# Keys' pieces on VectorE in one run, and the last batch's first maxima turned one event later

## The reference

```python
latent = x @ Wc_down
q = (latent @ Wq_up).reshape(Bsz, Tlen, N_HEAD, HEAD_DIM)
kv = latent @ Wkv_up
k, v = (kv[..., :HEAD_DIM], kv[..., HEAD_DIM:])
att = jnp.einsum('bthd,bsd->bhts', q, k) * scale
att = jnp.where(causal[None, None], att, -jnp.inf)
att = jax.nn.softmax(att, axis=-1)
y = jnp.einsum('bhts,bsd->bthd', att, v).reshape(Bsz, Tlen, C)
```

## Time and profile before

| | us |
|---|---|
| median of 3 runs | 868.62 |
| lowest, highest | 868.59, 870.29 |
| profiled execution | 868.64 |
| its span | 866.9 |

### The profile page before, as it was taken

The page is one execution under the profiler, slowest core; times in us unless marked ns, Lnnn a source line. Parts: engine busy times, 40 slices in busy tenths (PEclk is TensorE's granted clock), DMA queues, the critical chain, the costliest instruction groups (busy, mean ns, idle before and its releaser), DMA issues. The chain is left out here.

```text
span 866.9 us, 20372 instructions
## 1 busy us (share of the span) xinstructions
PE 812.4 (94%) x5472; PEld 487.5 (56%) x5473; DVE 641.0 (74%) x2159; ACT 548.7 (63%) x1236; POOL 294.8 (34%) x547
## 2 busy tenths in 40 slices
PE   7989999999999999999999999379999999999993
PEld 3433333333333333333333348279999999999993
DVE  7899888988898989898988628745555555555552
ACT  4636667867677777677776766146666666666661
POOL 5412333244233432441233322033444444444211
PEclk9989999999999999999999999579999999999997
DMA  6204222321211111111153118930000100110000
GB/s 209 71 11 112 77 81 97 100 86 64 97 55 57 48 36 58 62 42 43 64 172 113 52 57 268 330 96 31 30 31 31 36 30 27 36 32 19 19 19 2
DMA packets 55764, 62.92 MB, mean 73 GB/s; under 512 B 13166, under 2 KB 47366, under 8 KB 55568
## 3 DMA queue, kind: packets, MB, share of 16 engines
q1 hardware_dynamic: 51952, 53.71, 19.2%
q0 software_dynamic: 3744, 8.40, 3.1%
HBM read 36.12 MB, written 9.57 MB: 53 GB/s over the span
## 5 line engine op out<-in xcount | busy, mean ns | idle before, releaser
L1192 ACT ACTIVATE W2s<-bank 128x512 f32<-128x512 f32 (+1 forms) x512 | 257.1, 572 | 117.2 <-PE bank L1084 115.0
L1252 DVE CUSTOM_DVE_ANT_0 room_kv<-bank,causal 128x384 bf16<-128x384 f32 (+3 forms) x512 | 220.7, 486 | 31.9 <-PE bank L1053 30.5
L1084 PE MATMUL bank<-W2s,room_kv 99*128 99x512 bf16 (+3 forms) x768 | 224.2, 330 | 4.5 <-ACT W1s L1192 3.0
L1053 PE MATMUL bank<-room_kv,W2s 96*128 96x512 bf16 (+3 forms) x768 | 218.5, 330 | 4.3 <-DVE R L1223 2.7
L1255 DVE TENSOR_REDUCE MP<-bank 128x1 f32<-128x512 f32 x256 | 162.8, 681 | 12.5 <-PE bank L1053 12.4
L1400 POOL TENSOR_SCALAR_AFFINE_SELECT W2s<-W2s 128x512 f32<-128x512 f32 x96 | 60.9, 635 | 286.5 <-ACT W2s L1192 284.3
L1084 PEld LDWEIGHTS bank<-W2s,room_kv 99*128 99x128 bf16 x768 | 67.9, 97 | 146.0 <-ACT W2s L1192 62.3
L1667 PEld LDWEIGHTS hp<-XNT,LT 128*128 128x128 f32 x1248 | 147.3, 194 | 3.3 <-DVE XNT L1744 1.4
L1667 PE MATMUL hp<-XNT,LT 128*128 128x128 f32 x1248 | 147.8, 277 | 1.0 <-DVE XNT L1744 1.0
L1675 PE MATMUL yp<-W2s,LT 128*128 x624 | 141.2, 379 | 0.6 <-DVE z L1755 0.6
L1101 PE MATMUL bank<-W2s,room_kv 128*32 128x512 f32 (+2 forms) x1152 | 129.4, 534 | 0.1
(11 more groups left out here) (189 smaller groups left out, 760.2 us busy)
## 6 DMA issues: line engine op xcount, KB each, us to landing
W2s<-W2s SPq DMA_DIRECT2D x160, 64.0 KB, 2.6
W1s<-in_L_ffn_W_dram SPq DMA_DIRECT2D x8, 1024.0 KB, 5.5
W2s<-in_L_ffn_W_dram SPq DMA_DIRECT2D x8, 1024.0 KB, 7.3
Y<-in_L_attn_x_dram SPq DMA_DIRECT2D x8, 512.0 KB, 7.7
Y<-W1s SPq DMA_DIRECT2D x32, 128.0 KB
W1s<-den_rows SPq DMA_DIRECT2D x16, 256.0 KB
LT<-in_L_attn_x_dram SPq DMA_DIRECT2D x8, 512.0 KB, 7.7
x_rows<-LT SPq DMA_DIRECT2D x8, 512.0 KB, 5.2
```

What stands on the lines that cost most here:

```text
L1053: last = pe.matmul(bank[:, at:at + w], Q[0:NR, g, i // BW, h, i % BW * P:(i % BW + 1) * P], K[b % 2][0:NR, k * NQ:k * NQ + w], start=True, ...
L1084: last = pe.matmul(dst[:, i, :], K[b % 2][0:KR, j * P:(j + 1) * P], Q[0:KR, g, c, h, off:NQ], start=True, stop=True)
L1192: act.activation(PR[t % RB][:, heads[0]:heads[-1] + 1, off:NQ], unit_of(ST[(NU * n + u) % STB], s), ACT.Exp, scale=SCALE).then_inc(exp_don ...
L1252: op = dve.tensor_tensor_reduce(junk[:, done % 2, at:at + w], src, causal[:, NQ - w:NQ], 1.0, LOWEST, ALU.add, ALU.max, dst)
```

## The change

Two things are changed. For a keys' piece, VectorE does the residual at the piece's own event, straight behind the cast, instead of after the maximum that follows; the wait for its own cast moves behind the copy of the values. `DONE` counts the releases accordingly. And for the last batch (blocks 13, 14 and 15 as seen by the maxima, which run during blocks 12, 13 and 14), the first half's "m" is placed one event later in the table.

```diff
-            marks.append((NM * r + SET_LAST[c] + (MLAT if r else FIRST_MLAT[c]) + 0.5, ("m", r, c)))
+            marks.append((NM * r + SET_LAST[c] + (MLAT + (r > NG * (B - 1) and not c) if r else FIRST_MLAT[c]) + 0.5, ("m", r, c)))
...
-    if EVENTS[event][0] != "piece":
+    if EVENTS[event][0] != "piece" or EVENTS[event][2] == "k":
         DONE.append(event)
-    if event and EVENTS[event - 1][0] == "piece":
+    if event and EVENTS[event - 1][0] == "piece" and EVENTS[event - 1][2] != "k":
         DONE.append(event - 1)
...
             def residual(k):
                 _, b, name = EVENTS[k]
-                dve.wait_ge(part1, piece_no(b, name) + 1)
+                rows = rows_of(name)
                 dve.wait_ge(part3, piece_no(b, name))
-                rows = rows_of(name)
                 if name == "k":
                     dve.tensor_copy(R1[KEPT:KEPT + rows, :], ring[k % RING][0:rows, :]).then_inc(v_copied, 1)
+                dve.wait_ge(part1, piece_no(b, name) + 1)
                 dve.tensor_tensor(R1[0:rows, :], ring[k % RING][0:rows, :], parts(name)[0], ALU.subtract)\
                    .then_inc(ring_done, 1)
...
-                    if k and EVENTS[k - 1][0] == "piece":
+                    if (kind, b) == ("piece", "k"):
+                        residual(k)
+                    if k and EVENTS[k - 1][0] == "piece" and EVENTS[k - 1][2] != "k":
                         residual(k - 1)
```

## The result

| | kernel before | changed kernel |
|---|---|---|
| median, us | 868.59 | 863.80 |
| lowest, highest (5 runs each) | 868.11, 870.29 | 863.27, 865.36 |
| profiled execution, its span | 868.64, 866.9 | 863.80, 862.0 |

Over all sets of runs in this study the changed kernel's median is 864.5 (21 runs) and that of the kernel before 868.5 (72 runs), 4.0 us apart; why one set of five shows 4.8 and another 3.2 is most of what the experiments are about.

What follows compares the result with a forecast made beforehand. TensorE was taken to set the attention's pace. Keys' pieces 2.25 us plus last batch 1.30 us make 3.55, so 868.64 - 3.55 = 865.1 us; range 864.0 to 867.0 us.

Steps and rivals of the forecast that it cites:

- TensorE sets the pace of the attention, and what it gains is passed on: Attention part: TensorE idles less than any other engine, and everything behind the attention moves up as a whole.
- Keys' pieces, 2.25 us: Keys' piece in three batches: earlier subtraction frees the bank, transpose 0.95 us earlier, of which TensorE gains 0.75 each.
- the ends: Bounds of the gain per keys' piece: upper the full 0.95 us (2.85 together), lower 0.35 (1.05 together).
- VectorE's 0.35: Keys' piece: VectorE gains 0.35 us, all that counts if VectorE rather than TensorE sets the pace behind it.
- Last batch, 1.30 us: Last batch's three later transposes: work moved ahead fills 0.44, 0.42 and 0.44 us of TensorE's wait for GpSimd.
- The lower end of the range, 864.0: Whole kernel: time no lower than 864.0 us, the figure with both parts at their upper ends.
- rival 1: VectorE sets the pace behind the keys' piece: 1.05 + 1.30 = 2.35 us gained, 866.3 us; chance 0.11.
- rival 2: Last batch: the later transpose fills nothing, a matmul ahead of it waits instead; 2.25 us gained, 866.4 us; chance 0.06.
- rival 3: Keys' piece gains nothing lasting, through the displaced maximum's bank or a later wait; 1.30 us gained, 867.3 us; chance 0.11.
- Rival 4: Keys' pieces and last batch both reach their upper ends: 2.85 + 1.78 = 4.63 us gained, 864.0 us; chance 0.03.
- rival 5: Slower: new spacing brings a granted-clock fall of 1.72 us at each of three keys' pieces, 870.3 us; chance 0.05.

## Why the prediction was right in kind and too small

- **TensorE sets the pace of the attention, and what it gains is passed on.** Right. What the six places gained was still there at the last copy, and the experts' work moved up with it.
- **Keys' pieces, 2.25 us.** Right: 2.27. The order of starts came as worked out (copy 0.71 behind the cast, transpose 0.97 earlier against the cast, second matmul behind it late by 0.2), and so did the choice between the ends: TensorE leads, VectorE's 0.35 isn't what counts.
- **Last batch, 1.30 us.** The mis-sized term of the sum: 1.50. It priced the two matmuls that move ahead at 0.22 each, as the gap in front of a matmul of their own kind, and it put the transpose, had it not waited, 0.22 behind the maximum's matmul. But what moves up is the product with the values, and it stands 0.31 behind a maximum's matmul (417.25 to 417.56 in the kernel before) and only 0.15 behind a transpose (413.57 to 413.72). So 0.53 us are filled at the first and third place, measured 0.54 and 0.54. At the second, the transpose that no longer waits stands 0.31 behind the maximum's matmul, not 0.22, so its stall was 0.33 and not 0.42. From the maximum's matmul that was the last ahead of the transpose to the product it took 1.32 us (443.48 to 444.80) and now takes 0.91 (439.64 to 440.55): measured 0.40. That is near the 0.42 of the sum only because two errors nearly cancel: the stall was 0.09 us less, and the new order by itself saves 0.08.
- **The lower end of the range, 864.0: the step that failed.** The term of 0.20 alone would not have done it: with the measured 3.74 us the sum gives 864.9, inside the range. What failed is that the range put the clock at nothing on the way down. It took the profiled execution of 868.64 as its start and moved the terms of the edits alone in rivals 1 to 4; the clock entered only as rival 5, a fall that the change would bring. But the execution from which the sum starts itself held a fall, shown in the earlier trace rows, that some executions don't have and others have as a longer first fall, and the changed kernel's first profile is 1.05 us ahead of it before the first edited place. The changed kernel's first set had a median 0.7 us below its median over 21 runs. With 3.74 us and an estimate of a microsecond for the clock either way, from that 1.05, the range would have begun near 863.9, about where the result lies.
- **Rival 4** is nearest in time, 864.0, but by coincidence: its terms of 2.85 and 1.78 came as 2.27 and 1.50.
- **Rival 5** didn't come: no fall behind a shortened wait at 24 places, though a rare one isn't ruled out. The only one in this stretch stood behind the old, long wait.
- **Rivals 1, 2 and 3** are out, by 0.76 us at each keys' piece, still there at the end of the stretch, and 0.40 to 0.54 at each transpose.
- **Open:** whether the edits are worth more than 3.74 us. The pooled means are 4.1 us apart, by an estimate from the spread of the runs within 0.5 either way, which holds 3.74. Executions of equal mean clock are 4.2 (at 0.972) and 4.1 us (at 0.978) apart, within 0.3 either way, which leaves it just outside; but a mean doesn't say where in the kernel the clock fell. What share is the clock's sampling, and what a rare fall that the shorter wait prevents, isn't shown.

## What to carry to other kernels

Where a ring of buffers couples two engines, ask which event reuses the bank that is held longest, and let go of that bank first: the work that is put off costs only what its own bank's next user waits. When work is moved ahead of a wait, price it by the start of whatever then follows the wait, with the gap for that pair of instructions, not by the moved work's own spacing. And before summing on one profiled execution, read its granted clock from end to end, and compare it with a second profile of the same kernel: a fall that isn't in every execution belongs into the range on both sides, and one that is missing may stand elsewhere, here as a longer fall at 46 us.

## What the runs showed of the hardware

- The gap between two matmuls' starts depends on the pair: 0.22 to 0.23 us between the bf16 ones of 512 columns, 0.31 from one of these to the f32 product of line 1101 or to a transpose that doesn't wait (440.07 to 440.38), and 0.15 to 0.17 from the transpose to the matmul behind it.
- At the keys' pieces VectorE's gap from one 512-column instruction to the next is 0.60 to 0.61 or 0.70 to 0.72 us, and the order decides which. Behind a maximum the cast comes after 0.60 and the copy into R's partition 64 after 0.71 to 0.72, with the same length and bank. This is what the section "Two Vector instructions with no wait between them" in the Trainium skill's "VectorE: DVE Perf Modes" says of an output that begins in another group of 32 partitions; the trace agrees for the copy behind the maximum (0.71), the copy behind the cast (0.71), the subtraction behind the copy (0.71) and the cast behind the copy (0.72).
- The subtraction that waits for the cast just ahead of it stands 0.72 behind it, though both write from partition 0 on; behind a maximum on which it doesn't wait it stands 0.60.
- TensorE's granted clock fell from 2.4 to 1.2 GHz once behind a single wait of 1.34 us in otherwise dense work, and at the 17 other such waits it didn't. Identical kernels spread by 2 us, and up to 5 (867.1 to 872.2 in 12 runs). The falls differ between profiles of one kernel: near the start there was either a longer first fall (0.68 from 44 to 60 us) or a shorter one (0.79), the latter with or without a second fall at 68 us (0.57).
